# A two-layer graph network with routed experts: rows weighted inside the expert block and scattered with an add into one table in DRAM

## What is computed

```python
# L0: 8 experts, hidden 1024. The input is xt = layernorm(x); layer normalized again before the experts
top_p, top_idx = jax.lax.top_k(softmax(xt @ Wr + br), 2)
weights = top_p / top_p.sum(axis=-1, keepdims=True)
y = gelu(xe @ W1 + b1) @ W2 + b2                      # per expert
x = x + (weights[:, :, None] * sel).sum(axis=1)       # sel: y of the two chosen experts

# L1: 16 experts, hidden 512, input z = layernorm(x)
topk_w = jax.nn.softmax(topk_vals, axis=-1)
expert_out = relu(z @ w1 + b1) @ w2 + b2
y = z + sum_k topk_w[k] * expert_out[chosen k]
x = x + (y - mean(y)) / sqrt(var(y) + EPS) * gamma + beta
```

## Time and profile before

| | us |
|---|---|
| three runs: median (lowest to highest) | 2695.6 (2692.14 to 2705.16) |
| the profiled execution: its own time | 2695.01 |
| the profiled execution: span of its instructions | 2693.3 |
| PE busy (share of the span) | 2127.6 (79%) |
| DVE busy | 1651.9 (61%) |
| ACT busy | 1451.9 (54%) |
| POOL busy | 1396.2 (52%) |

### The profile page before, as it was taken

The page is one execution under the profiler, slowest core; times in us unless marked ns, Lnnn a source line. Parts: engine busy times, 40 slices in busy tenths (PEclk is TensorE's granted clock), DMA queues, the critical chain, the costliest instruction groups (busy, mean ns, idle before and its releaser), DMA issues. The chain is left out here.

```text
span 2693.3 us, 60550 instructions
## 1 busy us (share of the span) xinstructions
PE 2127.6 (79%) x15054; PEld 1744.7 (65%) x15055; DVE 1651.9 (61%) x4149; ACT 1451.9 (54%) x3568; POOL 1396.2 (52%) x1379
## 2 busy tenths in 40 slices
PE   4779966666767599999936889888885999679990
PEld 3666644444434499999924888787783777469990
DVE  8889963333333733333267877787877878843337
ACT  6779943333332443343346666666665888333335
POOL 0000067777777133333236777777752999236650
PEclk9989986767676699999967999999986999889995
DMA  3210036433333501111134787888863887552224
GB/s 114 96 58 21 22 89 198 137 106 106 105 105 101 202 32 35 35 37 37 41 110 149 242 240 238 247 242 240 241 199 107 268 269 240 191 183 70 70 66 147
DMA packets 181389, 365.89 MB, mean 136 GB/s; under 512 B 30058, under 2 KB 67348, under 8 KB 180990
## 3 DMA queue, kind: packets, MB, share of 16 engines
q1 hardware_dynamic: 118505, 208.65, 22.8%
q0 software_dynamic: 52608, 145.53, 19.6%
q10 hardware_dynamic: 10133, 9.97, 1.1%
HBM read 272.20 MB, written 91.83 MB: 135 GB/s over the span
## 5 line engine op out<-in xcount | busy, mean ns | idle before, releaser
L904 POOL DMA_INDIRECT weightsL_w<-y_gnn,all_slot_dst x416 | 396.0, 952 | 284.5 <-issue 282.7
L833 POOL DMA_INDIRECT scores_rows<-h_gnn,all_slot_dst x440 | 424.1, 964 | 141.7 <-issue 133.7
L963 PE MATMUL sum_ps<-weightsL_w 128*128 x880 | 341.9, 542 | 159.1 <-SPq L889 82.1
L963 PEld LDWEIGHTS sum_ps<-weightsL_w 128*128 128x128 f32 x880 | 217.4, 267 | 284.0 <-issue 250.4
L977 DVE TENSOR_TENSOR sums_acc<-sums_acc,sum_ps 128x256 f32 x440 | 185.5, 421 | 316.0 <-PE sum_ps L963 268.0
L1654 ACT ACTIVATE sums_acc<-expertsL_hid_ps,expertsL_b 128x128 f32<-128x128 f32 x704 | 197.6, 372 | 301.4 <-PE expertsL_hid_ps L1603 301.1
L1603 PE MATMUL expertsL_hid_ps<-sums_acc,expertsL_w 128*128 128x128 f32 x2816 | 337.4, 277 | 5.0 <-DVE sums_acc L1674 3.0
L2154 PE MATMUL scores_diff_ps<-all_ident,scores_rows 128*128 128x128 f32 x880 | 296.1, 337 | 48.1 <-DMA scores_rows<-h_gnn,all_slot_dst 40.3
L1603 PEld LDWEIGHTS expertsL_hid_ps<-sums_acc,expertsL_w 128*128 128x128 f32 x2816 | 327.2, 194 | 5.6 <-issue 5.5
L1615 PE MATMUL expertsL_out_ps<-weightsL_w,sums_acc 128*128 x1408 | 323.7, 380 | 0.0
L2156 PE MATMUL scores_diff_ps<-scores_minus,scores_node 128*128 128x128 bf16 x2640 | 309.6, 229 | 0.0
(11 more groups left out here) (456 smaller groups left out, 4235.1 us busy)
## 6 DMA issues: line engine op xcount, KB each, us to landing
saved_gnn<-scores_rows SPq DMA_DIRECT2D x220, 264.0 KB
sum_rows<-saved_gnn SPq DMA_DIRECT2D x220, 264.0 KB, 3.2
weightsL_w<-in_L_ffn_W SPq DMA_DIRECT2D x16, 1024.0 KB, 9.1
weightsL_w<-in_L_ffn_w SPq DMA_DIRECT2D x32, 512.0 KB, 9.8
scores_lanes<-slot_lanes SPq DMA_DIRECT2D x44, 320.0 KB
sort_low_b<-low_lanes SPq DMA_DIRECT2D x32, 416.0 KB, 4.5
weightsL_w<-ys_L SPq DMA_DIRECT2D x6, 1280.0 KB, 12.0
scores_rows<-h_gnn,all_slot_dst POOLq DMA_INDIRECT x440
```

The source lines that it names most:

```text
L833: pool.indirect_dma_start(out=self.rows[:, s, :], out_offset=None, in_=table[:, :], in_offset=bass.IndirectOffsetOnAxis(ap=e["slot_dst"][: ...
L904: pool.indirect_dma_start(out=rows[:, at:at + D], out_offset=None, in_=table[:, :], in_offset=bass.IndirectOffsetOnAxis(ap=e["slot_dst"][: ...
L963: last = nc.tensor.matmul(ps[(PAIRS * turn + s // 2) % len(ps)][:, s % 2 * D:(s % 2 + 1) * D], pick[h][:, s % HALF, :], rows[:, bass.ds(pl ...
```

## The change

The weighting of a row moves into its block and the addition over the two choices into the DMA. A table `sums` of 128 + 3,200 rows in DRAM takes the place of `ys_d`. It is begun as a copy of `x` (L0, from SBUF) or of `z_d` (L1, DRAM to DRAM). The weights are written by ACT's queue to a small DRAM table of 4-byte entries, and POOL gathers 128 of them for each block. Places of a block that hold no pair add zero rows to the first 128 rows of `sums`. At the end SP loads `sums` (3.3 MB, 6 DMAs), and DVE only takes the statistics. Core of the diff:

```diff
# route, SP (behind all weight loads of the layer)
                 for part in bring[ahead:]:
                     part(sp)
+                if again:
+                    sp.wait_ge(joined, NT)
+                    sp.dma_start(rows(r["sums"], 0, 1), x[:, 0:1, :]).then_inc(r["begun"], 16)
+                    sp.dma_start(rows(r["sums"], 1, NT + 1), x[:, :, :]).then_inc(r["begun"], 16)
+                else:
+                    sp.dma_start(r["sums"][0:P, :], z_d[0:P, :]).then_inc(r["begun"], 16)
+                    sp.dma_start(r["sums"][P:P + NR, :], z_d[:, :]).then_inc(r["begun"], 16)
# route, ACT, at its end
+                act.wait_ge(end, 1)
+                nc.scalar.dma_start(r["weights"][0:1, :], c["ones"][0:1, 0:1]).then_inc(r["weights_kept"], 16)
+                nc.scalar.dma_start(r["weights"][1:1 + TOP * NR, :].rearrange("(t p k) o -> p t (k o)", p=P, k=TOP), r["pairs"]).then_inc(r["weights_kept"], 16)
# experts, POOL
+                def bring_share(b):
+                    pool.indirect_dma_start(out=share[:, b:b + 1], out_offset=None, in_=r["weights"][:, :],
+                                            in_offset=bass.IndirectOffsetOnAxis(ap=slot[:, b:b + 1], axis=0)).then_inc(share_in[b % 2], 16)
                 for b in range(FEW):
                     bring(b)
+                pool.wait_ge(indices, 2)
+                pool.wait_ge(r["weights_kept"], 32)
+                for b in range(2):
+                    bring_share(b)
+                pool.wait_ge(r["begun"], 32)
...
-                    pool.indirect_dma_start(out=ys_d[:, :], out_offset=bass.IndirectOffsetOnAxis(ap=r["result"][:, b:b + 1], axis=0),
-                                            in_=yb[:, b % 2, :], in_offset=None).then_inc(y_out[b % 2], 16)
+                    pool.indirect_dma_start(out=r["sums"][:, :], out_offset=bass.IndirectOffsetOnAxis(ap=r["result"][:, b:b + 1], axis=0),
+                                            in_=yb[:, b % 2, :], in_offset=None, compute_op=ALU.add).then_inc(y_out[b % 2], 16)
+                    if b + 2 < NB:
+                        bring_share(b + 2)
# experts, DVE, shift
-                    ve.wait_ge(product, 2 + b + 1)
                     if count is not None:
                         ve.wait_ge(y_out[s], 16 * count)
+                    ve.wait_ge(share_in[s], 16 if count is None else 16 * count + 16)
...
-                    nc.vector.tensor_tensor(yb[:, s, :], out_ps[s][:, 0:D], b2_sb[:, bass.ds(ex * D, D)], ALU.add).then_inc(done, 1)
+                    nc.vector.tensor_scalar(yb[:, s, :], b2_sb[:, bass.ds(ex * D, D)], mine, None, ALU.mult)
+                    ve.drain()
+                    ve.wait_ge(product, 2 + b + 1)
...
+                    nc.vector.scalar_tensor_tensor(yb[:, s, :], out_ps[s][:, 0:D], mine, yb[:, s, :], ALU.mult, ALU.add).then_inc(done, 1)
# Results becomes Sums
+    def load(self, sp, n):
         tiles = self.PARTS[n]
+        sp.dma_start(self.target[:, tiles, :], rows(self.sums, 1 + tiles.start, 1 + tiles.stop)).then_inc(self.landed[n], 16)
+    def vector(self, ve, norm):
+        for n, tiles in enumerate(self.PARTS):
+            ve.wait_ge(self.landed[n], 16)
             for t in range(tiles.start, tiles.stop):
+                self.nc.vector.bn_stats(norm.stats[:, t, :], self.target[:, t, :])
```

More of the change, by code:

```diff
@@ L1193, in route @@
         norm = Norm(m, "ln")
-        if not again:
-            norm.scale, norm.shift = r["z_scale"], r["z_shift"]
         again_scale = m.sb("again_scale", [P, NT])
@@ L1731, in wait_landed @@
-    def wait_landed(self, eng, n):
-        eng.wait_ge(self.landed[n], 16 * len(self.pieces(n)))
-    def weigh(self, act, n):
-        self.wait_landed(act, n)
-        for tokens, tiles in self.pieces(n):
-            for t in range(tiles.start, tiles.stop):
-                mine = self.ys[0:tokens, t, 1, :]
-                op = self.nc.scalar.activation(mine, mine, ACT.Copy, scale=self.weight[0:tokens, 1, t:t + 1])
-        op.then_inc(self.weighed, 1)
-    def add_first(self, ve, n):
-        self.wait_landed(ve, n)
-        for tokens, tiles in self.pieces(n):
-            for t in range(tiles.start, tiles.stop):
-                mine = self.target[0:tokens, t, :]
-                self.nc.vector.scalar_tensor_tensor(mine, self.ys[0:tokens, t, 0, :], self.weight[0:tokens, 0, t:t + 1], mine, ALU.mult, ALU.add)
@@ L1805, in scalar @@
         self.nc.scalar.activation(self.norm.root[:, 0:1], self.c["ones"][:, 0:1], ACT.Sqrt)
-        for n in range(len(self.results.PARTS)):
-            self.results.weigh(act, n)
+        act.drain()
         self.norm.root_of_var(self.nc, act)
@@ L1869, in scalar @@
     def scalar(self, act):
[L1870 removed]
+        nc, z, norm = self.nc, self.z, self.norm
         nc.scalar.activation(norm.root[:, 0:1], self.c["ones"][:, 0:1], ACT.Sqrt)
[L1873 to L1882 removed]
+        act.drain()
         norm.root_of_var(nc, act)
```

109 lines of the change are left out of this document (38 added, 71 removed).

## The result

| | us |
|---|---|
| before: median of 4 runs (lowest to highest) | 2693.87 (2689.59 to 2705.16) |
| after: median of 4 runs (lowest to highest) | 2750.03 (2746.05 to 2751.95) |
| ratio, 95% interval | 1.0202 (1.0177 to 1.0226) |
| the profiled execution after: its own time, span | 2749.88, 2747.9 |

What follows compares the result with a forecast made beforehand. PE was taken to limit L1's blocks at 3.75 us, POOL close behind; after the change, the scatter's landing. Terms -18.8 - 19.8 + 1.5 + 8.4 + 51 + 3.2 + 1.6 = +27.1 on 2695.0 gave 2722 us; range 2676 to 2785.

Steps and rivals of the forecast that it cites:

- The ends: End of each layer: loading and statistics take 13.1 us, a gain of 18.8 us in L0 and 19.8 in L1.
- The weights' table: End of `route`: ACT's issue of 3,200 8-byte pieces takes 0.4 to 5 us; +1.5 us in L0, hidden in L1.
- The copy of z: Start of L1's blocks: a 15 us copy delays `b2` and the first scatter to about 2401, +8.4 us (bounds 2 and 12).
- POOL's issues: L1's loop: three indirect DMAs per block, 3 x (1.14 + 0.30) = 4.3 us, just below the landing's period.
- Rival D: The add is dear: landing above 4.2 us or scatter issue near 2 us, period 5.4 to 6.3, total 2770 to 2825; chance 0.18.
- The landing: L1's loop: the adding scatter lands in 3.5 us instead of 2.7; with its issue the period is 4.6 us, +51 us.
- Rival A: The forecast itself: the scatter's landing binds the loop at 4.45 to 5.3 us, total 2713 to 2765; chance 0.45.
- rival B: Landing grows by 0.3 us or less and POOL's issues bind at 4.1 to 4.4 us, total 2701; chance 0.20.
- The rule on the shared side of SBUF: L1's loop: DVE's multiply could lengthen one POOL issue per block by 0.3 us, period 4.6 us by POOL alone.
- The rule on the landing: Scatter's landing: 2.0 us plus bytes over 436 GB/s, so reading 128 KB more adds 0.3 us.
- L0 is covered: L0's loop: blocks of over 7 us cover POOL's at most 5.3 us; a block stage longer than 421 us would refute it.
- DVE's shift: L1's blocks: DVE's work per block, with about 0.4 us new, is 3.5 us, under the 4.6 us period.

Runs made afterwards that it cites:

- E3: Changed kernel with the weights' table written in 128 long pieces instead of 3,200 of 8 bytes: starts 22.7 us (L0), 25.8 (L1), ratio to before 1.0122.
- E11: E7 with the weights' table written in 3,200 pieces of 8 bytes: L0 start 30.2 us, ratio to before 0.9999.
- E9: E3 with L1's table begun early from rows of a weight input instead of the copy of z: L1 start 16.7 us; one run, 3086.4 us.
- E2: Changed kernel without the gathers of the weights (every row weighted by 0.5): L1 period 4.741 us, ratio to before 1.0178.
- E6: E2 without the weights' table, scatters alternating between two tables and waiting for the landing two blocks before: L1 period 3.776 us, ratio to before 0.9934.
- E5: E1 with DVE's shift as before the change, one addition of product and b2: L1 period 4.762 us, ratio to before 1.0188.
- E1: Changed kernel with a plain scatter that overwrites instead of adding: L1 period 4.704 us, ratio to before 1.0169.
- E7: The change in L0 alone, weights' table in long pieces, L1 as before the change: 3033.2 us against 3059.6, ratio to before 0.9941.
- E4: Changed kernel with neither the scatter's addition nor the gathers, and no weights' table: L1 period 3.721 us, ratio to before 0.9915.
- E10: E5 with the gathers still issued but DVE no longer waiting for them: L1 period 4.843 us; one run, 3113.5 us.
- E0: Changed kernel plus one register operation per PE wait in the aggregation, base of the experiments: L1 period 4.734 us, ratio to before 1.020.
- E8: Changed kernel, gathers kept, with adding scatters alternating between two tables: L1 period 4.712 us; one run, 3103.4 us.

## Why the prediction came out as it did

The direction was right and the total lies in the stated range, but the sum was 27.5 us short of the spans' +54.6: 12.0 at the starts of the blocks, 9.1 in L1's loop, 2.9 at the ends, 0.4 in L0's blocks and 3.1 outside all its terms. Two of the hits are in part luck, as said below. In its own steps:

- **The ends** (-18.8, -19.8): right, -18.1 and -17.6. In L1 the landing of parts was a little slower (DVE waited 2.88 us for the third part), in L0 the last 15 tiles ran through in 5.00 us, so that DVE kept up as forecast.
- **The weights' table** (+1.5, hidden in L1): this is the step that was most wrong for its size. It priced the issue, between 0.4 and 5 us, by the earlier trace rows, and the issue took 0.37. It did not price the landing, and "8 bytes drain faster than 1 KB" was wrong: from the issue of the 3,200 pieces to POOL's next step 13.6 us went by (930.94 to 944.55), with little else to move. They hold up `b1`, the fetches and `b2`: `b1` of L1 lands 18.7 us after its issue, and DVE's first copy, at 2390.41, stands behind it. E3 and E11 price the pieces at 8.2 to 9.7 us in L0 and E3 at 8.5 in L1, where they were said to be hidden.
- **The copy of z** (+8.4, bounds 2 and 12): the size was right, 9.1 us by E9, the mechanism half. `b2` was late, but so were `b1` and the first fetches: PE's first transpose is at 2382.70, 12 us behind the load of `b1`, where it came 5.3 us behind it before (2376.02 to 2381.29). The first scatter stands at 2401.00, where "about 2401" was forecast, but that is luck: L1's blocks begin 5.4 us sooner (by the load of `b1`), and the start took 14.0 us more and not 8.4. That the two causes add up to 8.5 + 9.1 = 17.6 us and the first chip shows 14.0 lies within the scatter of the starts.
- **POOL's issues** (4.3 us, "just below"): mis-sized. The forecast took the mean issue of 1.14 us for all three and looked for the price of the addition in the landing alone. The adding scatter also costs more to issue: 1.64 instead of 1.15 us in the loop, at best 1.59 instead of 0.97. With it 4.68 us. POOL is busy for 219.86 of 278 us, 79%, where the sign of being right was over 85%. Rival D had named such an issue, at a higher price.
- **The landing** (3.5 us, with the issue 4.65, period 4.6): right in kind, and close in size partly by luck. E2 gives 4.74 us with nothing else in the way, E6 takes the wait away and gets 3.78 us. But the sum of 1.15 + 3.5 counts the issue twice, since the 2.7 us of the earlier trace rows run from the issue's start: 2.7 + 0.8 would be 3.5 us from start to landing. By the same error the prediction held 3.85 us, "no shorter than the block", for a limit of the kernel before, where the landing came after 2.73. Measured are 3.83 us to the landing, as the issue too is longer, and 0.77 from there to the next start, which the sum does not have; together 4.6, and 4.74 in E2. The two errors nearly cancel. "Scatters 4.6 us apart released by the landing of the one before" holds for 25 of 57 in the changed kernel; the others are held by POOL's issues. Rival A (0.45) gave the number, and rival B's mechanism stands beside it; taking either away leaves the period where it is.
- **The rule on the shared side of SBUF.** The gather takes 1.18 us to issue in the loop and 0.95 at the start, so one issue a block is longer by 0.2 us. E5, where DVE's multiply is gone, has a median scatter issue of 0.99 us against 1.26 in E1. The Trainium skill, "SBUF — State Buffer", section "SBUF: two separate sides", says that GpSimd can't write descriptors while DVE runs such an operation in its two-port mode; both numbers agree with that.
- **The rule on the landing.** An estimate from "DMA: Bandwidth & Descriptors" of the Trainium skill, section "Anatomy of one DMA — SWDGE (gpsimd) path", had +0.3 us for 128 KB more to read. Measured from the issue's end the landing comes after 2.20 instead of 1.41 us, +0.8, which is what the prediction had allowed, and from its start after 3.83 instead of 2.73, +1.1: the measurement decides, the estimate is too low for a DMA that adds.
- **L0 is covered**: right. Its blocks and last landings take 2.0 us more, period 7.21 us where it was 7.18; E7 shows it from the other side. The stage as a whole is longer than 421 us, which was named as a refutation, but by its late start and not by its loop.
- **DVE's shift**: "3.5 us, under 4.6" was right, E4 runs at 3.72 us with it.
- **PE's idle share too small to matter**: right while POOL or the landing binds.

What stays open: why the gathers alone hold L1 at 4.7 to 4.8 us in E1, E5 and E10, where POOL's issues sum to 4.1 us or less and a landing is hardly waited for. The records show PE's groups completed late, by up to 8 us behind their modelled ends, with the signals of several groups close together, and PE stopping inside a group; they don't show what holds PE. DVE's new shift is excluded (E5), DVE's wait for the gather too (E10). Whether it is the 4-byte pieces written to SBUF or their number in POOL's queue was not tried. In the changed kernel itself no block shows this third hold (0 of 55, and 3, 1 and 4 in E0, E3 and E9); its 4.70 us are POOL's issues and the landing. But since every run that keeps the gathers and leaves out the addition or the wait for its landing (E1, E5, E8, E10) has the hold, no run shows what period POOL's three issues would give by themselves; their 4.68 us rest on the changed kernel's trace.

## What to carry to other kernels

Moving work from an end into a pipeline pays where the pipeline has room: in L0 (7.2 us a block, of which POOL needs some 5) the same edit gives 0.6% once the weights' table is written in long pieces (E7); in L1, where 3.75 us had to hold 4.7 us of POOL, it costs more than three times what L0 gives. Ask of each candidate limit what it would take alone, even if the trace shows no wait for it: here two limits of 4.7 us hid each other, and removing either one gave nothing. Check, too, from which end of an issue a view counts: the same landing is 2.7 us from the start and 1.4 from the end. And price a small DMA by its pieces and by its landing, not by its bytes or its issue: 25 KB in 8-byte pieces cost as much as the copy of 3.3 MB.
